# Down projection of a macaron block: two 256-column matmuls per tile of the hidden layer become one of 512 columns, and GpSimd adds the halves

## What is computed

```python
x = x + 0.5 * ffn(layernorm(x), w_gate, w_up, w_down)
x = x + attention(layernorm(x), Wq, bq, Wk, bk, Wv, bv, Wo, bo)
x = x + 0.5 * ffn(layernorm(x), w_gate, w_up, w_down)

def ffn(x, w_gate, w_up, w_down):          # w_gate, w_up: 704 x 256, w_down: 256 x 704
    h = silu(fp4_linear(x, w_gate)) * fp4_linear(x, w_up)
    return fp4_linear(h, w_down)

def fp4_linear(x, w):                      # both quantised in blocks of 16 along k, then multiplied
    return einsum("bsk,nk->bsn", fp4_quant_dequant(x), fp4_quant_dequant(w))
```

## Time and profile before

| | |
|---|---|
| median of 3 runs | 961.44 us (960.51 to 962.19) |
| profiled execution: time, span | 960.5 us, 958.7 us |
| TensorE matmuls busy | 920.2 us (96%), 6600 instructions |
| TensorE weight loads busy | 861.7 us (90%) |
| VectorE busy | 712.8 us (74%) |
| ScalarE busy | 657.3 us (69%) |
| GpSimd busy | 503.4 us (53%) |
| TensorE clock granted, mean | 0.996 of full |
| L1554 and L1561, matmuls | 600 and 420, median 279 to 280 ns each |
| L1163 down_out, ScalarE | 62, median 386 ns |
| L473 residual, GpSimd | 62, median 741 ns |
| L794 residual_last, VectorE | 2, 425 ns each |

### The profile page before, as it was taken

One profiled execution on the slowest core, in us unless ns is written; L12 is line 12 of the kernel. 1 busy time (PEld: TensorE's weight loads), 2 busy tenths in 40 slices (PEclk: granted clock), 3 DMA queues, 4 the chain that ended last, 5 costly groups with the idle time before them and its releaser, 6 DMA issues.

```text
span 958.7 us, 18223 instructions
## 1 busy us (share of the span) xinstructions
PE 920.2 (96%) x6600; PEld 861.7 (90%) x6600; DVE 712.8 (74%) x1187; ACT 657.3 (69%) x1384; POOL 503.4 (53%) x589
## 2 busy tenths in 40 slices
PE   3799999999989999999999999999989999999997
PEld 2678888889879899999999999999988888998987
DVE  7888988997767755566565545555577899999997
ACT  5767788888875776666657666666685765656654
POOL 3455667666530464444555544444483565666652
PEclk9999999999999999999999999999999999999999
DMA  9100000000000000000000000000000000000001
GB/s 318 41 1 1 1 1 1 2 1 1 1 1 1 2 1 2 1 2 2 1 2 1 1 2 1 2 1 1 2 1 1 1 24 23 23 23 24 1 23 44
DMA packets 11560, 13.94 MB, mean 15 GB/s; under 512 B 848, under 2 KB 10576, under 8 KB 11472
## 3 DMA queue, kind: packets, MB, share of 16 engines
q1 hardware_dynamic: 11472, 12.79, 4.0%
HBM read 8.59 MB, written 4.19 MB: 13 GB/s over the span
## 4 chain that ended last, share of the span: by engine, by line
PE 81%; DVE 10%; ACT 5%; issue 3%; POOL 1%; DMA 0%; SPq 0%; DVEq 0%; ACTq 0%
PE bank L1543 21%; PE bank L1795 18%; PE bank L1446 6%; PE bank_b L1554 6%; PE bank_b L1561 4%; PE bank_b L1843 3%; PE bank_b L1847 3%; PE bank L1843 3%; PE bank L1847 3%; PE bank_b L1845 3%; PE bank L1845 3%; PE bank L1750 2%; PE bank L1582 2%; DVE amax L682 1%; DVE grid L712 1%
## 5 line engine op out<-in xcount | busy, mean ns | idle before, releaser
L534 POOL TENSOR_TENSOR p_lo<-s_buf,p_hi 128x512 fp32r<-128x512 f32 x128 | 165.2, 1297 | 210.0 <-ACT p_hi L1345 201.9
L496 POOL TENSOR_TENSOR zq<-grid,s_neg 128x256 f32<-128x256 f32 (+2 forms) x184 | 172.7, 964 | 46.2 <-DVE grid L712 44.0
L1543 PE MATMUL bank<-w_hi,T_hi 128*128 128x512 f32 (+1 forms) x384 | 149.6, 390 | 4.2 <-DVE z L671 3.0
L1795 PE MATMUL bank<-q_hi,k_hi 128*128 128x256 f32 x512 | 145.2, 284 | 0.1
L1795 PE MATMUL bank<-q_lo,k_hi 128*128 128x256 f32 x512 | 144.8, 283 | 0.0
L1795 PE MATMUL bank<-q_hi,k_lo 128*128 128x256 f32 x512 | 144.8, 283 | 0.0
L1543 PE MATMUL bank<-w_hi,T_lo 128*128 128x512 f32 (+1 forms) x384 | 144.1, 375 | 0.0
L1543 PE MATMUL bank<-w_lo,T_hi 128*128 128x512 f32 (+1 forms) x384 | 143.7, 374 | 0.0
L1330 ACT ACTIVATE s_buf<-bank 128x512 f32<-128x512 f32 x128 | 76.3, 597 | 95.9 <-PE bank L1795 95.9
L1174 ACT ACTIVATE T_hi<-bank 128x1024 fp32r<-128x1024 f32 (+1 forms) x68 | 64.7, 952 | 86.3 <-PE bank L1446 86.3
L875 DVE TENSOR_TENSOR top<-bank,top 128x512 f32<-128x512 f32 x96 | 66.4, 692 | 65.8 <-ACT s_buf L1330 65.8
(11 more groups left out here) (219 smaller groups left out, 2584.8 us busy)
## 6 DMA issues: line engine op xcount, KB each, us to landing
out<-x SPq DMA_DIRECT2D x7, 512.0 KB, 3.0
x<-in_L_attn_hidden_states SPq DMA_DIRECT2D x3, 1024.0 KB, 13.9
x<-in_L_attn_hidden_states SPq DMA_DIRECT2D x2, 512.0 KB, 7.1
wraw<-in_L_ffn_w_down SPq DMA_DIRECT2D x1, 704.0 KB, 8.4
wraw<-in_L_ffn_w_gate SPq DMA_DIRECT2D x1, 640.0 KB, 4.7
wraw<-in_L_ffn_w_up SPq DMA_DIRECT2D x1, 640.0 KB, 5.8
wq_s<-in_L_attn_Wq SPq DMA_DIRECT2D x1, 512.0 KB, 8.0
wk_s<-in_L_attn_Wk SPq DMA_DIRECT2D x1, 512.0 KB, 8.8
```

The lines of the kernel that those rows point to most:

```text
L496: last = nc.gpsimd.tensor_tensor(out=blocks(zq[:, to:to + hi - lo]), in0=blocks(grid[:, lo:hi]), in1=spread(s_neg[:, par, lo // BLOCK:hi / ...
L534: nc.gpsimd.tensor_tensor(out=p_lo[:, n % 2, 2 * c:2 * c + 2, :], in0=score_buf(n, c), in1=p_hi[:, 2 * c:2 * c + 2, :].bitcast(F32), op=AL ...
L1543: last = nc.tensor.matmul(gu[:, lo:hi], lhsT=T[:, par, HK + kd, :], rhs=w[:, kd, lo:hi], start=n == 0, stop=n == len(terms) - 1)
L1795: last = nc.tensor.matmul(score_bank(c)[:, a, :], lhsT=kk[:, kd, t], rhs=q[:, n % 2, kd, :], start=i == 0 and a == 0, stop=i == len(terms) ...
```

## The change

The matmuls of T_hi take both halves of the weights at once, as 512 moving columns into the whole PSUM bank: 6 matmuls of 512 columns in place of 12 of 256, beside the 5 of T_lo (256 columns, into the first half as before). So the products with the upper and with the lower weights stand in two halves of the bank. `down_out` copies 512 columns. GpSimd adds the two halves to x one after the other, the second waiting for the first by the new semaphore x_half, and x_new is raised by the second. `residual_last` does the same on VectorE with last_half. Nothing else is edited. The diff, whole:

```diff
--- before.py
+++ after.py
@@ -114,7 +114,7 @@
         T_hi = sb("T_hi", [P, 2, HK + 1 + KD, P], F32R, at=ffn)
         T_lo = sb("T_lo", [P, 2, HK + KD, P], F32R, at=ffn)
         silu = sb("silu", [P, I], at=ffn)
-        down = sb("down", [P, 2, D], at=ffn)
+        down = sb("down", [P, 2, 2 * D], at=ffn)
         xjunk = sb("xjunk", [P, 4, D], at=ffn)
         wraw = sb("wraw", [P, NW * I], at=ffn)
         wy = sb("wy", [P, 2, I], at=ffn)
@@ -167,8 +167,8 @@
         flat5 = bank5[:].rearrange("p a n -> p (a n)")
         gu = flat5[:, 0:G]
         yabs = flat5[:, 3 * 512:3 * 512 + Z]
-        dn = bank_b[:, 0:D]
-        dn_last = bank4[:, 1, 0:D]
+        dn = bank_b[:]
+        dn_last = bank4[:, 1, :]
         wabs = (flat5[:, 3 * 512:3 * 512 + I], bank2[:].rearrange("p a n -> p (a n)")[:, 0:I])
         m_bank = bank4[:, 2, :]
         woT_bank = (bank_b[:], bank2[:, 0, :])
@@ -200,6 +200,7 @@
         T_done, hi_done, sub_done, lo_done = sem("T_done"), sem("hi_done"), sem("sub_done"), sem("lo_done")
         first_lo, late_hi, late_lo = sem("first_lo"), sem("late_hi"), sem("late_lo")
         dn_done, down_done, x_new, x_last = sem("dn_done"), sem("down_done"), sem("x_new"), sem("x_last")
+        x_half, last_half = sem("x_half"), sem("last_half")
         o_eps, o_rstd, o_nmr = sem("o_eps"), sem("o_rstd"), sem("o_nmr")
         xk_done, xk2_done, kT_done, khi_done, klo_done = (sem("xk_done"), sem("xk2_done"), sem("kT_done"),
                                                           sem("khi_done"), sem("klo_done"))
@@ -470,7 +471,10 @@
                 def residual(t, par):
 
                     pool.wait_ge(down_done, (NT - 1) * f + t + 1)
-                    nc.gpsimd.tensor_tensor(out=x[:, t, :], in0=x[:, t, :], in1=down[:, par, :],
+                    nc.gpsimd.tensor_tensor(out=x[:, t, :], in0=x[:, t, :], in1=down[:, par, 0:D],
+                                            op=ALU.add).then_inc(x_half, 1)
+                    pool.wait_ge(x_half, (NT - 1) * f + t + 1)
+                    nc.gpsimd.tensor_tensor(out=x[:, t, :], in0=x[:, t, :], in1=down[:, par, D:],
                                             op=ALU.add).then_inc(x_new, 1)
 
                 def scaled_x(k):
@@ -791,8 +795,13 @@
                 def residual_last():
 
                     dve.wait_ge(dn_done, NT * (f + 1))
-                    nc.vector.scalar_tensor_tensor(out=x[:, NT - 1, :], in0=dn_last, scalar=0.5, in1=x[:, NT - 1, :],
-                                                   op0=ALU.mult, op1=ALU.add).then_inc(x_last, 1)
+                    nc.vector.scalar_tensor_tensor(out=x[:, NT - 1, :], in0=dn_last[:, D:], scalar=0.5,
+                                                   in1=x[:, NT - 1, :], op0=ALU.mult,
+                                                   op1=ALU.add).then_inc(last_half, 1)
+                    dve.wait_ge(last_half, f + 1)
+                    nc.vector.scalar_tensor_tensor(out=x[:, NT - 1, :], in0=dn_last[:, 0:D], scalar=0.5,
+                                                   in1=x[:, NT - 1, :], op0=ALU.mult,
+                                                   op1=ALU.add).then_inc(x_last, 1)
 
                 def step(c, par):
                     blocks_of(c, par)
@@ -1549,17 +1558,17 @@
 
             def project_down_first(par, dn):
 
-                terms = [(k, half) for k in range(HK) for half in (0, D)]
-                for n, (k, half) in enumerate(terms):
-                    nc.tensor.matmul(dn, lhsT=T_hi[:, par, k, :], rhs=wd_hl[:, k, half:half + D],
-                                     start=n == 0, stop=False)
+                for k in range(HK):
+                    nc.tensor.matmul(dn, lhsT=T_hi[:, par, k, :], rhs=wd_hl[:, k, :], start=k == 0, stop=False,
+                                     skip_group_check=True)
 
             def project_down_rest(par, dn):
 
-                terms = [(T_hi, HK + KD, HK, half) for half in (0, D)] + [(T_lo, k, k, 0) for k in range(HK)]
-                for n, (T, k, wk, half) in enumerate(terms):
-                    last = nc.tensor.matmul(dn, lhsT=T[:, par, k, :], rhs=wd_hl[:, wk, half:half + D],
-                                            start=False, stop=n == len(terms) - 1)
+                nc.tensor.matmul(dn, lhsT=T_hi[:, par, HK + KD, :], rhs=wd_hl[:, HK, :], start=False, stop=False,
+                                 skip_group_check=True)
+                for k in range(HK):
+                    last = nc.tensor.matmul(dn[:, 0:D], lhsT=T_lo[:, par, k, :], rhs=wd_hl[:, k, 0:D],
+                                            start=False, stop=k == HK - 1, skip_group_check=True)
                 last.then_inc(dn_done, 1)
 
             def transpose_chain(f, c):
@@ -1665,18 +1674,18 @@
                     for k in range(HK):
                         if k == 4:
                             pe.wait_ge(hi_done, number(f, NT - 2 + par))
-                        for half in (0, D):
-                            nc.tensor.matmul(dn, lhsT=T_hi[:, par, k, :], rhs=wd_hl[:, k, half:half + D],
-                                             start=k == 0 and half == 0, stop=False)
+                        nc.tensor.matmul(dn, lhsT=T_hi[:, par, k, :], rhs=wd_hl[:, k, :], start=k == 0, stop=False,
+                                         skip_group_check=True)
 
                 def down_late_rest(par, dn):
 
-                    terms = [(T_lo, k, k, 0) for k in range(HK)] + [(T_hi, HK + KD, HK, half) for half in (0, D)]
-                    for n, (T, k, wk, half) in enumerate(terms):
-                        if n in (0, 4):
-                            pe.wait_ge(late_lo, 4 * f + 2 * par + 1 + n // 4)
-                        last = nc.tensor.matmul(dn, lhsT=T[:, par, k, :], rhs=wd_hl[:, wk, half:half + D],
-                                                start=False, stop=n == len(terms) - 1)
+                    for k in range(HK):
+                        if k in (0, 4):
+                            pe.wait_ge(late_lo, 4 * f + 2 * par + 1 + k // 4)
+                        nc.tensor.matmul(dn[:, 0:D], lhsT=T_lo[:, par, k, :], rhs=wd_hl[:, k, 0:D],
+                                         start=False, stop=False, skip_group_check=True)
+                    last = nc.tensor.matmul(dn, lhsT=T_hi[:, par, HK + KD, :], rhs=wd_hl[:, HK, :], start=False,
+                                            stop=True, skip_group_check=True)
                     last.then_inc(dn_done, 1)
 
                 return step, last_two
```

## The result

The changed kernel takes 965.22 us (median of 7 runs, 963.43 to 966.79); the kernel before, in runs beside it, 961.79 (7 runs, 960.51 to 963.73). The ratio is **1.0029, with a 95% interval of 1.0020 to 1.0039**: 2.8 us slower, at the edge of what can be told from no change. A second comparison gave 1.0026 [1.0015, 1.0037]. The forecast itself, "no change", didn't come: 965.2 lies above the 963.4 from which the prediction speaks of slower, a case to which it gave 0.23.

What follows compares the result with a forecast made beforehand. It took TensorE, never empty in both feed-forward passes, as the bound, VectorE close behind in FFN2. Terms -0.85 + 0.7 - 0.3 + 0.3 + 0.6 = +0.45 us on 961.44 gave 961.9 us; range 960.0 to 965.5.

Steps and rivals of the forecast that it cites:

- part 1: Down matmuls of each tile: 2.01 us become 1.97, 0.035 us less; -0.85 us in FFN1, -0.3 in FFN2's non-regular rounds.
- Weight loads: Faster rival: six loads of 0.188 us come off each TensorE round, giving about 932 us; chance 0.02.
- part 2: ScalarE's down_out copy goes from 0.39 to 0.60 us, +0.21, moving GpSimd's add later.
- part 3: Second GpSimd add, 0.74 us, starts 0.08 us behind s_neg, which goes through; price 0, upper bound 0.7 us a round.
- the nearer of two rows: FFN2: add 0.01 us ahead of s_neg lets it through; 0.13 us ahead stretches it to 0.74; the first was taken.
- The loop through copy, add and product: Regular FFN2 rounds: 13.87 us over two rounds, so 6.93 to 6.94 against 6.92 each; +0.3 us over 20 rounds.
- the 0.15 us of cover: Regular FFN2 rounds: TensorE starts 0.29 us after the product, could after 0.14; slightly too little for a 0.175 us delay.
- part 4: End of FFN1: second add holds L787 about 0.55 us, copy adds 0.21, matmuls save 0.04; +0.7 us.
- part 5: End of kernel: copy +0.21, second residual_last +0.46, three tiles of cheaper matmuls -0.1; together +0.6 us.
- the later add isn't covered: Slower rival: full 0.175 us reaches each regular FFN2 product, ends cost their upper bounds; about 964.7 us; chance 0.11.

Runs made afterwards that it cites:

- the pair with the bias row first: Kernel before and changed kernel, each with eight bias-row matmuls issued ahead of FFN1's last transposes: 959.29 us (0.9971) and 961.43 us (0.9990).

## Why the prediction came out as it did

**The matmuls (part 1).** Right to the digit: step 0.230, 1.97 us a tile. FFN1 gave 0.6 us where 0.85 was forecast: its 29 rounds take 209.8 to 210.0 us in the five profiles with before's matmuls and 209.3 to 209.4 in the nine with the wide ones. The four rounds that end with the product of tile 28 went from 28.60 to 28.48 us, 0.03 a round. The five rounds with statistics give nothing (8.24 us in both), as said; neither do the five right behind them (6.57), which the forecast had counted. Why not isn't shown.

**Weight loads.** That rival is refuted: 384 loads of 188 ns went and no regular round got shorter by more than the 0.035 us of the matmul steps. The step from start to start was the right thing to read, not the busy share of the loads. One sign, though, was misread: I wrote that TensorE's busy sum falls by some 65 us. The page's figure fell by 1.0 (920.2 to 919.2), because it is the time in which any matmul runs, and not the sum of durations that overlap. It couldn't have told anything either way. The rival's own sum was wrong by 1.6 us: 27 and 4 us off 961.44 are 930.4, not 932.

**The copy (part 2).** 0.60 us, as forecast.

**The second add (part 3).** The mechanism is confirmed from both sides: with the gap s_neg takes 0.21 us, without it 0.65. To take the nearer of two rows that point to opposite ends was right, and it was the most valuable decision of the prediction; the wrong one would have added 5 us in the regular rounds alone.

**The loop through copy, add and product: the step that failed.** The prediction found the loop (copy, add, s_up, product, TensorE's round), found that the 0.15 us of cover is slightly too little, and priced the round at 6.93 to 6.94 us. It measured 6.973, so 20 rounds cost 1.0 us and not 0.3. What it left out is in the timeline of the changed kernel: when TensorE has waited, its first matmul takes 0.31 us to the next one and not 0.23. Before, in the regular rounds, TensorE never waited, so its round (6.92, and 6.885 with the wide matmuls) held no such restart; as soon as the loop binds there is one in each round. It enters a loop that spans two rounds once: (13.87 + 0.08) / 2 = 6.975. With that term the other kernels come out as the loop says: the wide copy on before's matmuls, 6.975 + 0.035/2 = 6.99 (6.990 measured); without wide copy 6.885, TensorE's own (6.886); without the second add no change (6.975). The row for it was there to be read, in a round of FFN1 in which TensorE waited: its matmul is listed at 0.47 us where those of the earlier trace rows take 0.39. That is a term mis-sized, not a wrong mechanism: TensorE's stretch of the loop, put at 6.885 + 0.20, takes 0.08 us more. No run took the restart away and left the wait; it is shown by the steps (0.30 to 0.31 us in every regular round of the changed kernel, 0.23 in those of the kernels whose TensorE doesn't wait) and by the rounds that the loop gives with it.

**End of FFN1 (part 4).** L787 takes 0.74 us, so the +0.54 is right to the hundredth. In the pair without the clock's fall there the whole stretch costs 17.92 - 17.06 = +0.9 us against +0.7: the bounds were 0 and 1.4.

**End of the kernel (part 5).** +0.4 us between the profiles shown, +0.7 between the pair with the bias row first; +0.6 was forecast. The second residual_last stands bare at the end, 0.46 us.

**The sum.** In the pair with the bias row first: -0.55 (FFN1) + 0.86 (its end) - 0.11 (from there to the regular rounds) + 0.97 (19 regular rounds) + 0.70 (the end) = +1.9 us, against +2.1 by the medians and +1.8 by the ratios. The forecast had +0.45. Of the 1.4 between them 0.7 is the restart, 0.3 FFN1, 0.2 the end of FFN1, 0.1 the tail, and 0.2 the rounds ahead of the regular ones, which were to give 0.3 and gave 0.1 with a fall of the clock against them.

**The clock: not foreseen.** The profiled execution of before had the full clock at the end of FFN1, so nothing in its rows there spoke of it, and the prediction didn't ask what a TensorE that is empty for 2.57 us risks. (Its fall at the end of attention was there to be read.) At the end of FFN1 five profiles have a wait of 2.99 to 3.11 us, and all five show the lower clock behind it; five have 2.57 us, and three show it; the four with 0.84 to 1.36 us show none. Behind the 2.15 us at the end of attention, the same in every kernel, 10 of the 14 show it. At the end of FFN1 it costs 1.3 to 2.0 us: with a wait of 2.57 us the stretch takes 18.8 and 19.1 us at full clock, 20.5 to 20.8 with the fall. Since kernels with before's wait have it too, most of it lies in both sides of the comparison. What is left of the measured +2.8 (+2.5 in the second comparison) over the +1.9 of the sum could be a fall that comes more often or lasts longer behind a longer wait; five of five against three of five would fit that, but are too few to show it. That **stays open**: the interval of the ratio is as wide as this difference. For the number forecast the clock mattered in another way: the times of the 84 executions of before whose clock is on record go with their mean granted clock over the span (14 at 0.996 average 960.9 us, 36 at 0.993 average 962.9), and the profile on which the sum was built is one of the former. The mean doesn't say where the clock fell: the changed kernel's profile has 0.996 too. At equal mean clock the changed kernel's executions average 964.9 us (seven at 0.993), 2.0 more.

**The range.** That 965.2 us lies inside it is owed to the small slower rival, "the later add isn't covered" (964.7 us), for which the range was widened. This rival lies near the measured time for half of its reason: the later add is covered in part, as the loop says, and the restart and the ends made up the rest. And its sum isn't what its words say: 961.44 + 3.5 - 0.85 + 0.6 is 964.7, without the upper bound of 1.4 us for the end of FFN1; with it, it would be 966.1, outside the range. So the hit of the range is in part luck.

## What to carry to other kernels

Widening the moving side saves what the steps from start to start save, here 0.035 us in a tile of 1.97, and not what the number of instructions or of weight loads suggests; look for what the wider result costs behind it, the copy above all. When a change makes an engine wait that didn't wait before, add the engine's restart to the loop, and work out every loop that spans two rounds, with its restart, before calling a delay covered. A long wait on TensorE, here 2.57 us, is worth filling with independent matmuls: the moved work brought 1.7 us by itself, and the clock behind the wait, another 1.3 to 2.0 us, is at stake. Look at the granted clock behind every such wait before taking one profile for the kernel.

## What the runs showed of the hardware

- Who gets in when VectorE and GpSimd both want two SBUF operands was decided by hundredths: an operation behind a semaphore starts 0.08 us after the one that it depends on, and VectorE's s_neg (0.21 us) slips in between; a GpSimd operation that waits for nothing starts 0.05 us before the listed end of the one ahead, and s_neg takes 0.65. The Trainium skill, GPSIMD Engine Reference, section Specifications, tells that VectorE's instructions with two SBUF inputs contend with GpSimd; the traces agree (s_up 0.22 us alone, 0.48 behind the add of before, up to 0.60 behind the later one).
- A GpSimd add of 128x256 float32 into x takes 0.73 to 0.74 us; the doubling of `down`, with one tile as both inputs, 0.61, with a semaphore ahead of it or without. While L789, a VectorE operation with two SBUF operands of 704 elements, runs beside it, the add takes 1.25.
- A TensorE that has waited for a semaphore takes 0.31 us from its first 512-column matmul to the second, then 0.23.
- The granted clock was at its lower level (1.2 GHz) behind an empty stretch of 2.57 us in three profiles and at the full one in two, of kernels whose instructions of TensorE there are the same or nearly so, behind one of 2.15 us in 10 of 14, and in two behind one of 1.54 near the end of the kernel. Why it differs between them the traces don't tell.
